# Decoder layer on one core: self attention's short products moved between long ones, the context's transpositions ahead of the output's, the queries' transpositions into the next pass

## Chip, cores and metric

The kernel runs on one core of a Trainium2 chip. The metric is the device time of one execution in microseconds. The median of three runs of the kernel before is 750.39 us (744.05 to 751.88).

## What is computed

One decoder layer on x of 8 entries x 112 tokens x 256, with a context of 8 x 375 x 256: self attention, cross attention, and a mixture of experts, each added to its input and followed by a layer norm. The change lies in the two attentions. Self attention takes its softmax over the 112 tokens of an entry, 16 heads of width 16 with rotary positions; cross attention normalises x again, has 16 heads of width 64 and 375 keys, and its output is scaled by tanh of a gate.

```python
qkv = x @ qkv_w.T + qkv_b
q, k = rotary(q), rotary(k)
attn = softmax(einsum('abhqd,abhkd->abhqk', q, k) * hd ** -0.5)
out = einsum('abhqk,bhkd->abhqd', attn, v)
out = swapaxes(out, 1, 2).reshape(B, N, D) @ proj_w.T + proj_b
x = layernorm(x + out)
xn = layernorm(x, gamma, beta)
q = xn @ w_q
k, v = split(context @ w_kv)
attn = softmax(q @ k.T * DIM_HEAD ** -0.5)
x = layernorm(x + ((attn @ v) @ w_out + b_out) * tanh(gate))
x = layernorm(x + experts(x) + shared(x))
```

The rotary factors add a leading axis a of size 1, so the swap of axes 1 and 2 ahead of self attention's projection exchanges entries and heads. The 16 x 112 x 16 numbers of two heads over all eight entries thus become the 112 x 256 input of one entry's projection. The kernel follows this: what it calls the self attention of entry b is that of heads 2b and 2b + 1 over all entries, and its result goes through DRAM once to be laid out as rows.

## The kernel before

The program has three blocks, one after the other: the preparation (weights transposed and split into a high and a low part, q, k and v of self attention with rotary), the attention block, and the experts. Every product of two fp32 operands is made of three (high x low, low x high, high x high), so that six matmuls stand for one product over a width of 256 (`product`, lines 142 to 147).

The attention block works on one entry after the other. Before its loop the first entry's self attention is made. Then `iteration(b, more)` stands once for entry 0, in a hardware loop for entries 1 to 6, and once for entry 7, which has no next entry (`more` is false). I call one iteration a pass. It has eight stages s, one for each pair of heads of cross attention. In a stage PE has the scores of pair s (`scores`, into ps_s), the key projection of a later pair (`k_project`, into ps_kt), in six of the stages a projection of values (`v_project`, into ps_vx; which one, `V_AT` says), and the product of the probabilities of pair s - 2 with the values (`pv`, into ps_o). ACT copies k's high part out of PSUM (`k_hi`), takes the exponentials with their sums (`exps`), and makes the high part of the normalised probabilities of the pair before (`p_hi`). DVE takes the negated maxima (`maxima`, c_neg) and the low parts (`k_lo`, `v_lo`, `o_lo`). POOL normalises (`normalise`: a power, a product with a scale, and a product over 112 x 750) and makes the low part of the probabilities (`p_lo`). SyncE transposes them by DMA (`transpose_p`).

Into these stages the self attention of entry b + 1, its projection, its norms and its queries are filled in pieces, the fills. Their order and the stages are written out by hand in `FILLS` and `FILL_AT`: `FILL_AT[(s, n)]` names the fills that stand at place n of stage s. On PE place 0 is behind the scores, place 1 behind the key projection, place 2 behind the value projection, place 4 behind `pv`. Every engine runs through the same table (`place(n)` in each `iteration`) for its part of a fill: PE makes it (`fill`), ACT copies or exponentiates (`fill_hi`), DVE takes maxima, low parts or moments (`fill_lo`). The fills are

- QA, QB, KA, KB: transpositions of stacked queries and keys of self attention; S0 to S3: its scores; T0 to T3: transpositions of its exponentials (128 x 112 tiles, in the profile ps_a<-ident,work);
- O0, O1: its output, 16 short matmuls each of 34 or 18 columns (ps_a<-v_self,pt_hi and pt_lo, lines 1245 and 1246), which need the low parts that DVE writes (`pt_lo`, from `self_pt`);
- OT: transposition of the output, which goes through DRAM to be laid out anew (`store_o`, `load_o` on SyncE); PJ: its projection; C0, C1: transpositions of the next context (`ctx_transpose`);
- NT: transposition of the normed x (xn); R0, R1: the query projection; Q0, Q1: transpositions of the queries (q_rows).

All fills write one of two PSUM banks (ps_a) in turn; `free(name, b)` has PE wait until the fill two places back in `FILLS` has been read. The semaphores are counted, so a fill that is moved waits for the same counts. Between PJ and NT lie two norms: DVE takes moments of x plus the output (`residual_moments`, count n1), POOL the power -0.5 (`rsqrt`), DVE norms and takes moments again (`x1_moments`, n2), POOL the second power, DVE writes xn (`xn_norm`, line 949). ACT then makes xnt_f and xnt_hi from NT (`xn_affine`, `xn_hi`), DVE the low part.

The order on every engine is that of the code. Besides the fills, the change touches the places of `store_o`, `load_o`, `load_ctx` and `load_x` on SyncE, of `residual`, `rsqrt` and `x1_out` on POOL, of `xn_hi` on ACT, and of `x1_moments`, `xn_norm` and `chunk_max` on DVE. `chunk_max` is the largest magnitude in a chunk of the experts' weights, loaded in the loop's shade.

Of the kernel before, what the change touches and what calls it, by code (L numbers as in the profile page):

```python
# [439 lines left out]
def attention_block(nc, sg, A, x2_all, ident, consts, weights, qk_rot, v_all, raw, ffn_sg, w_max, gw_raw, xs, v_cols):  # L440
# [3 lines left out]
    with ExitStack() as ctx:  # L444
# [96 lines left out]
        def _(sp):  # L541
# [62 lines left out]
            for b in range(B):  # L604
                more = b + 1 < B
                for s in range(PAIRS):
# [5 lines left out]
                    if more and s == 2:  # L612
                        store_o(b + 1)
                        load_o(b + 1)
                    if more and s == 5:
                        load_chunk(3 * b + 2)
                    if b + 2 < B and s == 5:
                        load_ctx(b + 2)
                        load_x(b + 2)
# [6 lines left out]
        def _(pool):  # L626
# [66 lines left out]
            def iteration(b, more):  # L693
                for s in range(PAIRS):
# [3 lines left out]
                    if more and s == 6:  # L698
                        rsqrt(rstd[:, 1:2], mv[:, 1, :], "n2", b + 2)
                    if s >= 1 or later(b):  # L700
                        late_p_lo(b, s)
                    normalise(b, s)
                    if more and s == 5:
                        rsqrt(rstd[:, 0:1], mv[:, 0, :], "n1", b + 2)
                    if more and s == 1:
                        residual(b + 1)
                    if more and s == 6:
# [8 lines left out]
        def _(act):  # L716
# [168 lines left out]
            def iteration(b, more):  # L885
                for s in range(PAIRS):
# [4 lines left out]

                    if more and s == 0:
# [13 lines left out]
                    place(1)  # L906
                    if s not in (1, 2, 3, 7):
# [16 lines left out]
                    if more and s == 6:  # L924
                        xn_hi(b + 1)
# [6 lines left out]
        def _(dve):  # L932
# [197 lines left out]
            def iteration(b, more):  # L1130
                for s in range(PAIRS):
                    def place(n):
                        if more:
                            for f in FILL_AT.get((s, n), ()):
                                if f != "NT":
                                    fill_lo(b + 1, f)

                    if more and s == 6:
                        x1_moments(b + 1)
                    maxima(b, s)  # L1140
                    if more and s == 6:
                        xn_norm(b + 1)
                    if more and s == 7:
                        fill_lo(b + 1, "NT")
# [19 lines left out]
                    if more and s == 7:  # L1164
                        chunk_max(3 * b + 2)
# [9 lines left out]
                    if more and s == 4:  # L1175
                        chunk_max(3 * b + 1)
                    place(4)
                    if s == 2 and later(b):
# [11 lines left out]
        def _(pe):  # L1190
            def free(name, b):

                i = FILLS.index(name)
                if name in ("PJ", "NT"):
# [61 lines left out]
            def ctx_transpose(b, k):  # L1256
                pe.wait_ge(sg["ctx_loaded"], 16 * (b + 1))
                if later(b):
# [3 lines left out]
                    else:  # L1262

                        pe.wait_ge(sg["ot_lo"], b + 1)
# [136 lines left out]
            def iteration(b, more):  # L1401
                for s in range(PAIRS):
# [6 lines left out]
                    if s == 0:  # L1409
                        k_project(b, 2)  # L1410
                    scores(b, s)
# [8 lines left out]
                    if s != 2 and s in V_AT and (s < 6 or more):  # L1420
# [728 lines left out]
```

## Time and profile before

| | |
|---|---|
| median of the runs | 750.39 us |
| profiled execution | 752.2 us |
| its span, first to last instruction | 750.4 us |
| mean granted TensorE clock | 0.876 |
| PE busy | 583.8 us (78%) |
| DVE, ACT, POOL busy | 453.9, 412.9, 379.7 us |
| scores of entry 0's first pair | from 109.5 us |
| last scores of the loop | at 545.8 us |

The attention loop takes the middle of the span; the preparation stands before it, the experts behind. A row of a timeline is: start, duration, engine, line, operation, output<-inputs, shape, count, and in brackets the idle time of the engine just before, with what ended it. PE's durations are longer than the distance between two starts, since matmuls are pipelined; the distance is what one costs.

### The profile page before, as it was taken

Reading aid. Unit: us, or ns where it says so; the run is one execution under the profiler, and the core shown is the slowest. Engines: PE = TensorE matmul, PEld = TensorE weight load, DVE = VectorE, ACT = ScalarE, POOL = GpSimd, SP = SyncE. Lnnn points to the kernel's source line nnn. Section 1 sums busy time; section 2 is a strip of 40 time slices with the busy share of each in tenths; the row PEclk is TensorE's granted clock in tenths of the full one; section 3 lists DMA queues with packets and bytes.
Section 4 is the critical chain, followed back from the end, with each engine's and each line's share of the span. In section 5 each row is a group of like instructions: output and inputs, shape, how many; then the busy total and the mean of one; then the engine's idle time right before and its main releaser. Section 6 shows DMA issues by size and latency. Waiting matters only on the chain. (4 is left out here: it accounts for less than half of the span.)

```text
span 750.4 us, 13691 instructions
## 1 busy us (share of the span) xinstructions
PE 583.8 (78%) x4362; PEld 447.3 (60%) x4362; DVE 453.9 (60%) x837; ACT 412.9 (55%) x991; POOL 379.7 (51%) x426
## 2 busy tenths in 40 slices
PE   4734677888889888988888888887436777899990
PEld 3523555767767767767767767766335454566650
DVE  3894346567667668667677567664426766833332
ACT  2434247568558568468577577564325554744431
POOL 3452026567467577477476577566541560233332
PEclk9965588989989999899999899999755899999995
DMA  8625112354353353354354344336545466533324
GB/s 220 215 89 175 27 41 66 64 97 95 67 110 83 77 110 87 73 110 110 56 104 117 62 91 111 67 74 172 128 112 202 124 214 240 127 57 58 58 35 106
DMA packets 146135, 79.37 MB, mean 106 GB/s; under 512 B 105331, under 2 KB 135283, under 8 KB 146099
## 3 DMA queue, kind: packets, MB, share of 16 engines
q1 hardware_dynamic: 141714, 72.92, 39.2%
q0 software_dynamic: 4384, 5.99, 4.8%
q8 instruction: 20, 0.33, 0.2%
q14 instruction: 17, 0.13, 0.1%
HBM read 46.74 MB, written 10.13 MB: 76 GB/s over the span
## 5 line engine op out<-in xcount | busy, mean ns | idle before, releaser
L680 POOL TENSOR_TENSOR p<-probs,p 112x750 f16<-112x750 f32 x64 | 100.5, 1571 | 64.1 <-ACT p L718 64.1
L674 POOL TENSOR_TENSOR probs<-probs,c_rcp 112x750 f32<-112x750 f32 x64 | 92.0, 1438 | 5.0
L821 ACT ACTIVATE probs<-ps_s,c_neg 112x375 f32<-112x375 f32 x128 | 72.2, 573 | 26.7 <-DVE c_neg L1043 26.5
L718 ACT ACTIVATE p<-probs 112x750 f16<-112x750 f32 x64 | 53.1, 830 | 50.1 <-POOL probs L674 50.1
L1630 POOL DMA_INDIRECT moe_sum<-gsh_hi,xs_in x21 | 33.3, 1586 | 85.6 <-ACT gsh_hi L1681 69.9
L670 POOL TENSOR_TENSOR c_rcp<-c_sum,neg_one 112x2 f32<-112x2 f32 x64 | 45.2, 706 | 59.0 <-ACT probs L821 58.7
L1043 DVE TENSOR_REDUCE c_neg<-ps_s 112x2 f32<-112x750 f32 x64 | 59.6, 932 | 12.4 <-PE ps_s L147 12.0
L1943 PE MATMUL ps_h<-w_ex,xst_hi 128*128 (+1 forms) x168 | 57.8, 386 | 2.8 <-DVE xst_lo L1720 2.7
L935 DVE TENSOR_TENSOR kt_lo<-ps_kt,kt_hi 128x376 fp32r<-128x376 f32 x64 | 34.9, 546 | 35.3 <-ACT kt_hi L718 35.3
L1038 DVE SCALAR_TENSOR_TENSOR v_lo<-ps_vx,v_scale,v_hi 128x512 f16<-128x512 f32 (+1 forms) x48 | 36.0, 750 | 33.4 <-ACT v_hi L813 33.3
L145 PE MATMUL ps_kt<-ctxt_hi,w_k_lo 128*128 128x376 f32 x128 | 53.7, 420 | 0.0
L1342 PE MATMUL ps_o<-p_t,v_lo 128*64 128x112 f16 (+1 forms) x384 | 37.0, 231 | 15.7 <-DMA p_t<-p 9.3
L147 PE MATMUL ps_kt<-ctxt_hi,w_k_hi 128*128 128x376 f32 x128 | 47.3, 369 | 0.0
L146 PE MATMUL ps_kt<-ctxt_lo,w_k_hi 128*128 128x376 f32 x128 | 47.3, 369 | 0.0
L145 PE MATMUL ps_s<-kt_hi,qt_lo 64*112 64x376 f32 x128 | 29.4, 448 | 20.5 <-ACT probs L821 17.0
L813 ACT ACTIVATE v_hi<-ps_vx,v_scale 128x512 f16<-128x512 f32 (+1 forms) x48 | 33.1, 689 | 21.2 <-PE ps_vx L147 21.1
L145 PE MATMUL ps_vx<-w_v_hi,ctxt_lo 128*128 128x512 f32 (+1 forms) x96 | 43.9, 457 | 0.6 <-DVE res L1053 0.6
L718 ACT ACTIVATE kt_hi<-ps_kt 128x376 fp32r<-128x376 f32 x64 | 30.5, 477 | 24.7 <-PE ps_kt L147 23.3
L1867 DVE TENSOR_TENSOR gsh_hi<-ps_g,gsh_hi 128x512 f16<-128x512 f32 x21 | 14.5, 690 | 47.2 <-ACT gsh_hi L1675 47.2
L1342 PEld LDWEIGHTS ps_o<-p_t,v_lo 128*64 128x64 f16 (+1 forms) x384 | 22.8, 115 | 31.4 <-DMA p_t<-p 18.6
L1083 DVE TENSOR_REDUCE w_max<-chunk 128x1024 f32 (+1 forms) x27 | 32.7, 1212 | 14.3 <-DMA chunk<-in_L_ffn_sw_dram 9.8
L146 PE MATMUL ps_vx<-w_v_lo,ctxt_hi 128*128 128x512 f32 (+1 forms) x96 | 41.2, 430 | 0.0
(307 smaller groups left out, 1805.6 us busy)
## 6 DMA issues: line engine op xcount, KB each, us to landing
chunk<-in_L_ffn_ew_dram SPq DMA_DIRECT2D x24, 512.0 KB, 3.9
spare<-in_L_ffn_ew_dram SPq DMA_DIRECT2D x18, 512.0 KB, 6.5
store<-in_L_ffn_ew_dram SPq DMA_DIRECT2D x6, 512.0 KB, 5.2
ctx_all<-in_ctx_dram SPq DMA_DIRECT2D x2, 1500.0 KB
ctx_raw<-in_ctx_dram SPq DMA_DIRECT2D x8, 375.0 KB
moe_in<-chunk SPq DMA_DIRECT2D x1, 2709.0 KB, 14.9
plain_raw<-in_L_xattn_w_kv_dram SPq DMA_DIRECT2D x2, 1024.0 KB, 15.9
xs_in<-moe_in SPq DMA_DIRECT2D x15, 129.0 KB
```

Of the source, the lines that this page charges most:

```text
L145: eng.matmul(out, ll, rh, start=start, stop=False, **kw)
L146: eng.matmul(out, lh, rl, start=False, stop=False, **kw)
L147: return eng.matmul(out, lh, rh, start=False, stop=stop, **kw)
L670: pool.tensor_tensor(c_rcp[:, s % 2, :], c_sum[:, s % 2, :], neg_one[:, :], ALU.pow).then_inc(sg["c_rcp_part"], 1)
L674: pool.tensor_tensor(probs[:, s % 2, :, :], probs[:, s % 2, :, :], c_rcp[:, s % 2, :].unsqueeze(2).to_broadcast([N, 2, SK]), ALU.mult).the ...
L680: pool.tensor_tensor(p16[:, s % 2, 1, :, 0:SK], probs[:, s % 2, :, :], p16[:, s % 2, 0, :, 0:SK], ALU.subtract)\
L718: return act.activation(dst, src, ACT.Copy)
L821: act.activation(probs[:, s % 2, h, :], ps_s[0:N, h, 0:SK], ACT.Exp, bias=c_neg[:, s % 2, h:h + 1], accum_out=c_sum[:, s % 2, h:h + 1]).th ...
L1038: dve.scalar_tensor_tensor(v[1][0:n, q, t, :], ps_v[0:n, :], v_scale[0:n, 0:1], v[0][0:n, q, t, :], op0=ALU.mult, op1=ALU.subtract).then_i ...
L1043: dve.tensor_reduce(c_neg[:, s % 2, :], ps_s[0:N, :, 0:SK], X, ALU.max, negate=True).then_inc(sg["c_neg_ready"], 1)
L1342: last = pe.matmul(ps_pv[h * CHD:(h + 1) * CHD, :], v[a][0:n_k, s // 4, t, at:at + CHD], p16_t[0:n_k, s % 2, (2 * w + h) * ST + t, :], sta ...
L1943: last = pe.matmul(out, lhs[a], rhs[b], start=start and n == 0, stop=stop and n == 2)
```

## The change

The table moves O0, T2, T3 and O1 one or more places later, puts both context transpositions at one place of stage 5, OT behind `pv` of that stage, PJ into stage 6, NT into stage 7, R0 and R1 to the end of stage 7, and takes Q0 and Q1 out of it. Those two now stand in stage 0 of the next pass, behind its key projection, and V02 follows them, ahead of the scores. The second context transposition waits for the bank's reader before it in the new order (pt_lo), and OT for the context's low parts. `store_o` and `load_o` move from stage 2 to 3 on SyncE, the loads of context and x from 5 to 6; the residual moves from stage 1 to 4 on POOL, and the norms' steps move on POOL, DVE and ACT with PJ and NT.

```diff
-           (2, 1): ["S2", "S3"], (2, 2): ["T0"], (2, 3): ["T1"], (3, 0): ["O0", "T2"],
-           (3, 1): ["T3"], (3, 2): ["O1"], (5, 1): ["OT", "C0"], (5, 4): ["C1", "PJ"],
-           (6, 4): ["NT"], (7, 2): ["R0", "R1"], (7, 4): ["Q0", "Q1"]}
+           (2, 1): ["S2", "S3"], (2, 2): ["T0"], (2, 3): ["T1"], (3, 1): ["O0", "T2"],
+           (3, 2): ["T3"], (4, 0): ["O1"], (5, 1): ["C0", "C1"], (5, 4): ["OT"], (6, 1): ["PJ"],
+           (7, 1): ["NT"], (7, 4): ["R0", "R1"]}
...
-                    if more and s == 2:
+                    if more and s == 3:
                         store_o(b + 1)
                         load_o(b + 1)
...
-                    if b + 2 < B and s == 5:
+                    if b + 2 < B and s == 6:
                         load_ctx(b + 2)
...
-                    if more and s == 6:
+                    if more and s == 7:
                         rsqrt(rstd[:, 1:2], mv[:, 1, :], "n2", b + 2)
                     if s >= 1 or later(b):
                         late_p_lo(b, s)
+                    if more and s == 6:
+                        rsqrt(rstd[:, 0:1], mv[:, 0, :], "n1", b + 2)
                     normalise(b, s)
-                    if more and s == 5:
-                        rsqrt(rstd[:, 0:1], mv[:, 0, :], "n1", b + 2)
-                    if more and s == 1:
+                    if more and s == 4:
                         residual(b + 1)
-                    if more and s == 6:
+                    if more and s == 7:
                         x1_out(b + 1)
...
+                    if s == 0 and later(b):
+                        fill_hi(b, "Q0")
+                        fill_hi(b, "Q1")
...
                     place(1)
+                    if more and s == 7:
+                        xn_hi(b + 1)
...
-                    if more and s == 6:
-                        x1_moments(b + 1)
+                    if s == 0 and later(b):
+                        fill_lo(b, "Q0")
+                        fill_lo(b, "Q1")
                     maxima(b, s)
-                    if more and s == 6:
+                    if more and s == 7:
                         xn_norm(b + 1)
...
+                    if more and s == 6:
+                        x1_moments(b + 1)
                     place(4)
+                    if more and s == 7:
+                        chunk_max(3 * b + 2)
...
+                if name == "OT" and later(b):
+                    pe.wait_ge(sg["ctxt_lo"], 2 * b + 2)
...
-                        pe.wait_ge(sg["ot_lo"], b + 1)
+                        pe.wait_ge(sg["pt_lo"], 4 * b + 4)
...
                     if s == 0:
                         k_project(b, 2)
+                        if later(b):
+                            fill(b, "Q0")
+                            fill(b, "Q1")
+                        v_project(b, V_AT[0])
                     scores(b, s)
```

Three places show what moves. The first is DVE from stage 3 to stage 4 of a pass in the loop. pt_lo are the low parts of T2 and T3, s_rcp is the first step behind O1, c_neg the maxima of the next stage's scores. Before:

```order
L966 REGISTER_ALU
L935 TENSOR_TENSOR pt_lo<-ps_a,pt_hi 112x448
L1031 REGISTER_ALU
L935 TENSOR_TENSOR kt_lo<-ps_kt,kt_hi 128x376
L935 TENSOR_TENSOR pt_lo<-ps_a,pt_hi 112x448
L1036 REGISTER_ALU
L1038 SCALAR_TENSOR_TENSOR v_lo<-ps_vx,v_scale,v_hi 128x512
L972 REGISTER_ALU
L977 RECIPROCAL s_rcp<-ps_a 112x8
```

And now:

```order
L969 REGISTER_ALU
L938 TENSOR_TENSOR pt_lo<-ps_a,pt_hi 112x448
L1039 REGISTER_ALU
L1041 SCALAR_TENSOR_TENSOR v_lo<-ps_vx,v_scale,v_hi 128x512
L938 TENSOR_TENSOR pt_lo<-ps_a,pt_hi 112x448
L938 TENSOR_TENSOR oct_lo<-ps_o,oct_hi 128x112
L1046 TENSOR_REDUCE c_neg<-ps_s 112x2
L975 REGISTER_ALU
L980 RECIPROCAL s_rcp<-ps_a 112x8
```

T3's low part, which O1 needs, now stands behind the low part of V11, and O1's reading behind the maxima of stage 4.

The second is DVE from PJ's moments on: mv is the last step of a set of moments, x the first norm, xn the second. Before, in stages 5 and 6:

```order
L1002 TENSOR_TENSOR res<-ps_a,x_res 112x256
L939 BN_STATS stats<-res 112x6
L942 BN_AGGR mv<-stats 112x2
L944 TENSOR_SCALAR mv<-mv 112x1
L949 TENSOR_SCALAR x<-res,mv,rstd 112x256
```

And now, in stages 6 and 7:

```order
L947 TENSOR_SCALAR mv<-mv 112x1
L1039 ISA
L1041 SCALAR_TENSOR_TENSOR v_lo<-ps_vx,v_scale,v_hi 128x512
L938 TENSOR_TENSOR oct_lo<-ps_o,oct_hi 128x112
L952 TENSOR_SCALAR x<-res,mv,rstd 112x256
```

The first norm stands behind the low parts of a value projection and of a pair's output.

The third is PE at the start of a pass: ps_s are the scores of stage 0, ps_vx is V02, work are QA and QB. Before:

```order
L147 MATMUL ps_s<-kt_hi,qt_hi 112x376
L1312 ISA
L145 MATMUL ps_vx<-w_v_hi,ctxt_lo 119x512
L146 MATMUL ps_vx<-w_v_lo,ctxt_hi 119x512
L147 MATMUL ps_vx<-w_v_hi,ctxt_hi 119x512
L145 MATMUL ps_vx<-w_v_hi,ctxt_lo 119x512
L146 MATMUL ps_vx<-w_v_lo,ctxt_hi 119x512
L147 MATMUL ps_vx<-w_v_hi,ctxt_hi 119x512
L1208 ISA
L1214 MATMUL ps_a<-ident,work 128x112 x4
```

And now:

```order
L1293 REGISTER_ALU
L1296 MATMUL ps_a<-ident,q_rows 128x112 x8
L1317 ISA
L145 MATMUL ps_vx<-w_v_hi,ctxt_lo 119x512
L146 MATMUL ps_vx<-w_v_lo,ctxt_hi 119x512
L147 MATMUL ps_vx<-w_v_hi,ctxt_hi 119x512
L145 MATMUL ps_vx<-w_v_hi,ctxt_lo 119x512
L146 MATMUL ps_vx<-w_v_lo,ctxt_hi 119x512
L147 MATMUL ps_vx<-w_v_hi,ctxt_hi 119x512
L1326 REGISTER_ALU
L1329 REGISTER_ALU
L145 MATMUL ps_s<-kt_hi,qt_lo 112x376
```

V02 stands ahead of the scores of stage 0 and behind the transpositions of the queries, so that nothing but QA, QB and `pv` is left between those scores and KA.

## Rows read from the trace of the kernel before

**Rows 1.** Windows of passes: length, busy per engine, PEclk, DMA share, GB/s.

```profile
280.50:335.60 55.10, 48.80 (x416) 39.71 (x416) 39.19 (x71) 37.56 (x104) 36.46 (x41) 0.94 0.43 91
335.60:390.30 54.70, 47.38 (x416) 38.06 (x417) 39.00 (x71) 37.53 (x104) 36.41 (x41) 0.97 0.43 89
...
sum 335.20, PE 294.98 PEld 238.22 DVE 234.07 ACT 226.47 POOL 219.03; mean PE 49.16 PEld 39.70 DVE 39.01 ACT 37.74 POOL 36.50
```

**Rows 2.** Waits of PE over six passes: sum in us, times, longest.

```profile
PE ps_a L1279 <- DVE xn L949: 14.0, 6, 2.4
PE ps_a L1245 <- DVE pt_lo L935: 7.2, 11, 1.0
PE ps_o L1342 <- DMA p_t<-p: 4.7, 4, 1.5
PE ps_a L1266 <- DVE ot_lo L935: 3.8, 5, 1.6
PE ps_a L1214 <- ACT q_stacked_t L739: 2.8, 6, 0.5
PE ps_s L145 <- DVE qt_lo L935: 2.8, 6, 0.6
```

**Rows 3.** Window in stages 3 and 4 of one pass, same columns.

```profile
301.00:307.80 6.80, 6.80 (x28) 6.05 (x27) 3.83 (x9) 2.57 (x7) 1.54 (x4) 0.50 0.31 68
```

**Rows 4.** Timeline of PE, stages 3 and 4: starts of O1, pv, sc, kp, V12, pv.

```profile
307.70 0.23 PE L1245 MATMUL ps_a<-v_self,pt_hi 112*112 112x34 f32 x1
...
309.34 0.24 PE L1342 MATMUL ps_o<-p_t,v_lo 128*64 128x112 f16 x2
...
309.91 0.43 PE L145 MATMUL ps_s<-kt_hi,qt_lo 64*112 64x376 f32 x2
...
310.61 0.44 PE L145 MATMUL ps_kt<-ctxt_hi,w_k_lo 128*128 128x376 f32 x1
...
311.74 0.40 PE L145 MATMUL ps_vx<-w_v_hi,ctxt_lo 128*119 128x512 f32 x1
...
313.24 0.24 PE L1342 MATMUL ps_o<-p_t,v_lo 128*64 128x112 f16 x2
```

**Rows 5.** Timeline of PE and DVE at the start of stage 3.

```profile
298.33 0.43 PE L145 MATMUL ps_s<-kt_hi,qt_lo 64*112 64x376 f32 x2
...
298.43 0.74 DVE L1038 SCALAR_TENSOR_TENSOR v_lo<-ps_vx,v_scale,v_hi 128x512 f16<-128x512 f32 x1
299.08 0.61 DVE L935 TENSOR_TENSOR pt_lo<-ps_a,pt_hi 112x448 fp32r<-112x448 f32 x1
...
301.25 0.93 DVE L1043 TENSOR_REDUCE c_neg<-ps_s 112x2 f32<-112x750 f32 x1
```

**Rows 6.** Timeline of ACT, from exps of stage 4 to exps of stage 5.

```profile
312.32 0.57 ACT L821 ACTIVATE probs<-ps_s,c_neg 112x375 f32<-112x375 f32 x1
...
313.42 0.69 ACT L813 ACTIVATE v_hi<-ps_vx,v_scale 119x512 f16<-119x512 f32 x1
...
316.21 0.83 ACT L718 ACTIVATE p<-probs 112x750 f16<-112x750 f32 x1 [1.95 <-POOL probs L674]
316.95 0.47 ACT L718 ACTIVATE kt_hi<-ps_kt 128x376 fp32r<-128x376 f32 x1
...
317.91 0.59 ACT L821 ACTIVATE probs<-ps_s,c_neg 112x375 f32<-112x375 f32 x1
```

**Rows 7.** Timeline of DVE and POOL in stage 6: the two norms.

```profile
322.33 0.41 DVE L949 TENSOR_SCALAR x<-res,mv,rstd 112x256 f32<-112x256 f32 x1 [0.80 <-POOL rstd L661]
...
323.75 0.56 POOL L661 TENSOR_TENSOR rstd<-mv,const_neg_half 112x1 f32<-112x1 f32 x1 [1.53 <-DVE mv L944]
324.28 1.56 POOL L680 TENSOR_TENSOR p<-probs,p 112x750 f16<-112x750 f32 x1
...
324.44 1.55 DVE L949 TENSOR_SCALAR xn<-x,mv,rstd 112x256 f32<-112x256 f32 x1
```

**Rows 8.** Timeline of PE in stage 0: the scores, and KA.

```profile
335.64 0.43 PE L145 MATMUL ps_s<-kt_hi,qt_lo 64*112 64x376 f32 x2 [0.46 <-DVE qt_lo L935]
...
339.81 0.41 PE L1214 MATMUL ps_a<-ident,work 112*128 112x112 f32 x2 [0.48 <-ACT q_stacked_t L739]
```

More of the change, by code:

```diff
@@ L923, in iteration @@
                     place(4)
-                    if more and s == 6:
-                        xn_hi(b + 1)
             iterations(act, iteration)
@@ L1134, in place @@
                             for f in FILL_AT.get((s, n), ()):
-                                if f != "NT":
-                                    fill_lo(b + 1, f)
-                    if more and s == 6:
-                        x1_moments(b + 1)
+                                fill_lo(b + 1, f)
+                    if s == 0 and later(b):
+                        fill_lo(b, "Q0")
+                        fill_lo(b, "Q1")
                     maxima(b, s)
-                    if more and s == 6:
+                    if more and s == 7:
                         xn_norm(b + 1)
-                    if more and s == 7:
-                        fill_lo(b + 1, "NT")
                     place(0)
@@ L1163, in iteration @@
                         v_lo_cross(b if s < 6 else b + 1, V_AT[s])
-                    if more and s == 7:
-                        chunk_max(3 * b + 2)
                     if s != 2:
@@ L1419, in iteration @@
                         cross_out(b - 1)
-                    if s != 2 and s in V_AT and (s < 6 or more):
+                    if s not in (0, 2) and s in V_AT and (s < 6 or more):
                         v_project(b if s < 6 else b + 1, V_AT[s])
```

## The prediction

> **What bounds the kernel now.** I read the windows of the attention loop's passes first, then the waits of PE inside the loop, then the timelines around the longest ones. One pass of the loop handles one batch entry and takes 335.20 / 6 = 55.87 us over six of them; PE is busy 49.16 us of it, more than any other engine, so PE sets the time and each of its waits lies on the path [rows 1]. PE loses time in two ways. It waits: the reader is to see six waits that the change touches, 14.0 + 7.2 + 4.7 + 3.8 + 2.8 + 2.8 = 35.3 us in six passes, 5.88 us a pass [rows 2]. And its clock falls: granted 0.97 in the pass that took 54.70 us, 0.94 in the mean, and 0.50 (1.2 GHz) for 6.8 us in stage 3, where PE had just waited and then run the many short products of self attention's output [rows 1, 3]. At half speed a stretch loses at most half of itself, so a pass loses at most 0.06 x 55.87 = 3.4 us to the clock.
>
> In the words below sc is a stage's scores, kp the key projection, V a value projection, pv the product with the probabilities; "stage" is one of the eight pairs of heads. At 2.4 GHz, from start to start: sc 0.70, kp 1.13, V 1.50, pv 0.57, one self output (O0 or O1) 1.64 us [rows 4].
>
> The second thing to see is a chain beside PE, the softmax of each pair. ACT runs exps, POOL normalises, ACT copies p, then k_hi, then the next exps: 312.32, 316.21, 316.95, 317.91, a step of 5.59 us in stage 5, where two small copies stand in it, and about 5.0 without them (316.95 + 0.4 - 312.32) [rows 6]. Eight steps of 5.0 are 40 us, less than a pass, so today the chain has room; but the room is in the first stages, and whatever is placed ahead of kp delays k_hi and with it the exps queued behind it on ACT.
>
> **The change part by part.** PE's instructions are the same in number and form; no engine's work is removed. So only waits and the clock can change, and I work out each wait, all in us after the start of sc in stage 3.
>
> 1. *O0 behind kp, T3 behind V11, O1 in stage 4.* O0's wait for pt_lo goes, since kp's 1.13 stands in front of it: part of the 7.2 / 6 = 1.20. O1 now needs T3's pt_lo. DVE's maximum of stage 3 ends at 302.18, 3.85 after sc [rows 5]; then ACT has exps (1.10 to the next instruction [rows 6]), T2's copy (an estimate of 0.5 from pt_lo's 0.61, the same tile on DVE) and v_hi 0.69, DVE v_lo 0.74 and pt_lo 0.61 [rows 5, 6]. The sum is 7.5. PE is ready for O1 after sc, kp, O0, T2, V11, T3, pv, sc = 0.70 + 1.13 + 1.64 + 0.45 + 1.50 + 0.45 + 0.57 + 0.70 = 7.1 (T2 and T3 estimated at 0.45 each). O1 waits 0.4 to 0.5: 1.20 becomes 0.5.
>
> 2. *O1 ahead of kp in stage 4, C0 and C1 ahead of exps in stage 5.* O1 ends at 7.5 + 1.64 = 9.2, kp at 10.3, k_hi at 10.8: only then exps of stage 4. One step later, with both context copies in it (5.7), exps of stage 5 starts at 16.5 and ends at 17.6; sc of stage 6 needs it. PE's work after O1 is kp, V, pv, sc, kp, C0 and C1 (0.75, estimated), pv, OT (0.2) = 6.55, done at 15.7. The wait, in front of OT and sc together, is 1.9. What goes: the context's wait for ot_lo, 3.8 / 6 = 0.63, and the wait for the transposed p in front of pv, 4.7 / 6 = 0.78, because SyncE now issues the transposition of p ahead of the store of the output that it had stood behind. Both are covered by the new wait. If the chain were ahead, they would be gains: bounds 0 and 1.9 for the new wait; I take 1.9, since the step of 5.59 is measured and PE has 2 us too little work to fill it.
>
> 3. *PJ in stage 6, NT in stage 7.* Both move by the same two blocks (sc and kp), so the wait of NT, 14.0 / 6 = 2.33, changes only by what its chain gains or loses. The next exps (stage 6) starts at 21.5, ends at 22.6; sc of stage 7 waits 0.25 for it. PJ's moments on DVE now stand behind k_lo, which waits for k_hi (ends 21.5) and takes 0.5: they run from 22.1 and take 1.4, as x does with its moments up to POOL's rstd (322.33 to 323.75) [rows 7]. POOL's rsqrt then stands ahead of its normalisation of stage 6, and the second rsqrt behind it: 23.5 + 0.6 + 2.7 (316.21 - 312.32 less 1.10 [rows 6]) + 0.56 [rows 7] = 27.4, then xn. For xn the rows have two prices: 1.55 where POOL's p runs beside it (324.28 to 325.84), 0.41 for the same form, x, with POOL idle [rows 7]. Behind the second rsqrt POOL's p must first get its copy from ACT (0.83 [rows 6]), so I take 0.41 and keep 1.55 for the range. NT at 27.8; PE is there at 22.6 + 0.70 + 1.13 = 24.4. The wait is 3.4, for 2.33 before. The Trainium skill, SBUF — State Buffer, section Who interferes with whom, says that GpSimd and a VectorE tensor_scalar in a two-port mode share one port pair, that the first to issue holds it for its whole instruction and that the other blocks fully. By that rule xn goes first here and 0.41 holds, as the 1.55 beside p and the 0.41 beside an idle POOL suggest; were p first, each pass would be 1.1 us longer and the total some 8 us. R0 had no wait of its own; ACT now has p, k_hi and exps of stage 7 (0.74 + 0.4 + 1.1) ahead of NT's copies and PE only V and pv (2.07) to cover it, where sc, kp and V (3.33) did. Bounds 0 and 2.2; I take 0.8.
>
> 4. *Q0 and Q1 in the next pass, V02 ahead of sc of stage 0.* The wait for qt_lo goes: 2.8 / 6 = 0.47. But KA waits for QA's copy, and on ACT that is queued behind exps of stage 0 and v_hi. From sc to KA the trace has 335.64 to 339.81, 4.17 us, with V02's 1.50 inside and a wait of 0.48 [rows 8]. ACT's part of it stays; V02 leaves. The wait becomes 0.47 + 1.50 = 2.0, bounds 1.5 (if qt's copies run earlier than the scores) and 2.5 (if ACT, which now starts the stage with them, is late by their 1 us).
>
> 5. *The rest* (residual, loads of context and x, x1_out, the moved chunk maximum) lies on POOL, SyncE and DVE with stages to spare. I cost it at nothing; its cover is that the data are read a stage or more later. If the context came late, PE would wait for it in stage 5.
>
> **The sum.** Waits touched before: 5.88 a pass. After: 0.5 + 1.9 + 0.25 + 3.4 + 0.8 + 2.0 = 8.85. That is 3.0 more a pass. The clock: two thin stretches stand apart now, which helps, but there are three waits of 1.9 to 3.4 us where there was one of that length, and the trace shows 0.50 behind such places. I leave its loss as it is, 3.4 at most, with ends of none (3.0 - 3.4 = -0.4) and half as much again (+4.7). Seven passes fill the next entry: 7 x 3.0 = 21 us. On the profiled execution's 752.2 us (span 750.4 and 1.8 around it) that gives 773; the median of the runs shown is 750.39, 1.8 lower, so I forecast 771.
>
> **The rivals.** *The clock wins* (faster). If the softmax chain keeps ahead of PE in stages 4 to 6, so that the 1.9 and the extra 1.1 at NT don't appear, the waits come out even (5.9 for 5.88) and the dense products around O0 and O1 give back most of the clock's loss, say 2.5 of 3.4: 7 x 2.5 = 17 us less, 733 on the median. The fall to 0.50 just in stage 3 speaks for it; against it speaks that from the end of kp in stage 4 the chain needs 0.5 + 5.7 + 1.1 = 7.3 us to the end of the next exps, and PE has 6.55 - 1.13 = 5.4 of work. It decides as soon as exps of stage 4 starts before about 9 us after sc of stage 3. Chance 0.19. *A wash* (no change): the waits come as worked out, the clock's loss goes: 7 x -0.4, 748, up to 757. Chance 0.16. *Worse*: xn beside p (8 us) and the clock lower behind the three waits: above 786. Chance 0.07, part of slower. *The change doesn't do what it says*: the order of PE shows O0 between kp and V and Q between kp and V02; it does.
>
> **How the numbers follow.** The forecast itself, 757 to 786, has 0.58. With the worse case slower has 0.65; about 1% (7.5 us) is what a measurement of this kernel can tell from no change; same 0.16; faster 0.19. The range goes from 737, which takes in the wash and the weaker half of the clock's case, to 786.
>
> **What would show it.** In the changed profile: PE waits of about 2 us in front of KA (on ACT's q_stacked copy), about 3 in front of NT (on xn), 1.5 to 2 in front of OT or sc of stage 6 (on ctxt_lo or exps), and none on p_t, ot_lo or qt_lo; passes of 58 to 60 us; xn at 0.4. The forecast is wrong if passes fall under 55 us with a granted clock near 1, or if the exps of stage 4 starts within 9 us of sc of stage 3.

## The result, and the profile after

The changed kernel takes 770.81 us in the median of four runs (765.25 to 775.25), beside 751.13 for the kernel before (744.05 to 753.02): a ratio of 1.0276, with a 95% interval of 1.0181 to 1.0371. It is slower, by 1.8 to 3.7%. Measured again beside the experiments it gave 1.0304 (1.0225 to 1.0382).

| | before | after | after, again |
|---|---|---|---|
| profiled execution | 752.2 us | 765.25 us | 774.06 us |
| its span | 750.4 us | 763.4 us | 772.2 us |
| mean granted clock of the span | 0.876 | 0.866 | 0.856 |
| mean of six passes of the loop | 55.87 us | 57.92 us | 59.12 us |

The windows of passes (length, busy time per engine, PEclk, DMA share, GB/s) of the changed kernel answer to [rows 1]:

```profile
167.90:225.70 57.80, 49.83 (x418) 40.07 (x418) 38.63 (x71) 37.77 (x103) 36.35 (x41) 0.91 0.40 89
341.80:399.20 57.40, 49.93 (x416) 40.29 (x416) 38.76 (x71) 37.83 (x103) 36.24 (x41) 0.91 0.40 88
...
sum 347.50, PE 299.05 PEld 240.29 DVE 232.06 ACT 226.13 POOL 217.54; mean PE 49.84 PEld 40.05 DVE 38.68 ACT 37.69 POOL 36.26
```

347.50 / 6 = 57.92 us a pass, 2.05 more than before. Seven times that is 14.4 us, and the two profiled executions are 13.0 apart: the whole difference lies in the loop. The granted clock is 0.91 in every pass; in the kernel before it is 0.91 in two of the six passes, 0.94 in three and 0.97 in one. PE stands idle for 57.92 - 49.84 = 8.08 us of a pass, 1.37 more than before (55.87 - 49.16, [rows 1]), and is busy 0.68 us longer with the same matmuls: in this profile two thirds of the loss are waits, and one third is the lower clock. PE's waits over the six passes (sum in us, times, longest), to be laid beside [rows 2]:

```profile
PE ps_a L1284 <- DVE xn L952: 14.1, 6, 2.9
PE ps_a L1219 <- ACT q_stacked_t L739: 9.7, 6, 1.7
PE ps_a L1258 <- DMA o_rows<-o_shuffle: 8.0, 4, 2.0
PE ps_a L145 <- DVE xnt_lo L938: 4.0, 6, 1.2
PE ps_a L1250 <- DVE pt_lo L938: 2.9, 6, 0.5
PE ps_a L1258 <- issue: 2.9, 2, 1.4
...
PE ps_s L145 <- DVE qt_lo L938: 1.9, 6, 0.4
PE ps_s L145 <- ACT probs L821: 1.3, 5, 0.3
```

L1284 is NT, L1219 KA, L1258 OT, L145 with xnt_lo R0, L1250 O1. The waits for p_t and ot_lo are gone, the one for pt_lo has shrunk from 7.2 to 2.9, and three have come: 10.9 us in front of OT (two rows), 9.7 in front of KA (2.8 before), 4.0 in front of R0.

The row of OT has to be read with care. It names the DMA of o_rows in four passes and nothing ("issue") in two. The timeline of one pass, from sc of stage 3: exps of stage 4 on ACT, the context's low parts on DVE, OT on PE, and further on xn and NT:

```profile
360.53 0.43 PE L145 MATMUL ps_s<-kt_hi,qt_lo 64*112 64x376 f32 x2
...
371.30 0.57 ACT L821 ACTIVATE probs<-ps_s,c_neg 112x375 f32<-112x375 f32 x1
...
376.89 0.99 DVE L938 TENSOR_TENSOR ctxt_lo<-ps_a,ctxt_hi 128x375 fp32r<-128x375 f32 x2
...
377.99 0.38 PE L1258 MATMUL ps_a<-ident,o_rows 112*128 112x112 f32 x2 [2.00 <-DMA o_rows<-o_shuffle]
...
387.94 0.42 DVE L952 TENSOR_SCALAR xn<-x,mv,rstd 112x256 f32<-112x256 f32 x1 [0.21 <-POOL rstd L661]
...
388.40 0.37 PE L1284 MATMUL ps_a<-ident,xn 112*128 112x112 f32 x1 [2.01 <-DVE xn L952]
```

ctxt_lo ends at 377.88 and OT starts 0.11 later. The load of o_rows was issued at 375.60 and the view of the DMA issues gives it 1.9 us to land, that is 377.5. The bank that OT writes, freed by ctxt_lo, came last; the DMA was only 0.4 us ahead of it. In the two passes with "issue" PE's clock fell to 0.50 behind O1's wait; there the exps of stage 4 and OT come a microsecond later. Where a wait has two causes, the row names one, and the ends of both have to be looked up.

### The profile page after: what moved, and what is told of

The parts are those of the page before. It is cut to its first block and busy times, and to the rows that moved or that the text cites. A ratio compares the mean times of both kernels' runs of the same rounds, so it can differ in the third digit from the quotient of the medians.

```text
span 763.4 us, 13709 instructions
## 1 busy us (share of the span) xinstructions
PE 586.5 (77%) x4362; PEld 448.0 (59%) x4362; DVE 451.3 (59%) x837; ACT 412.3 (54%) x991; POOL 378.4 (50%) x426
## 5 line engine op out<-in xcount | busy, mean ns | idle before, releaser
L718 ACT ACTIVATE p<-probs 112x750 f16<-112x750 f32 x64 | 53.3, 832 | 72.3 <-POOL probs L674 72.3
L670 POOL TENSOR_TENSOR c_rcp<-c_sum,neg_one 112x2 f32<-112x2 f32 x64 | 44.8, 700 | 56.8 <-ACT probs L821 56.3
L1046 DVE TENSOR_REDUCE c_neg<-ps_s 112x2 f32<-112x750 f32 x64 | 59.6, 931 | 12.1 <-PE ps_s L147 11.9
L1952 PE MATMUL ps_h<-w_ex,xst_hi 128*128 (+1 forms) x168 | 57.9, 387 | 2.8 <-DVE xst_lo L1729 2.7
L145 PE MATMUL ps_kt<-ctxt_hi,w_k_lo 128*128 128x376 f32 x128 | 53.6, 418 | 0.0
L1041 DVE SCALAR_TENSOR_TENSOR v_lo<-ps_vx,v_scale,v_hi 128x512 f16<-128x512 f32 (+1 forms) x48 | 35.9, 748 | 24.4 <-ACT v_hi L813 24.4
L145 PE MATMUL ps_vx<-w_v_hi,ctxt_lo 128*128 128x512 f32 (+1 forms) x96 | 44.9, 468 | 0.6 <-DVE res L1056 0.6
L145 PE MATMUL ps_s<-kt_hi,qt_lo 64*112 64x376 f32 x128 | 29.0, 441 | 20.9 <-ACT probs L821 18.7
L147 PE MATMUL ps_vx<-w_v_hi,ctxt_hi 128*128 128x512 f32 (+1 forms) x96 | 42.5, 442 | 0.0
L1086 DVE TENSOR_REDUCE w_max<-chunk 128x1024 f32 (+1 forms) x27 | 32.7, 1210 | 14.1 <-DMA chunk<-in_L_ffn_sw_dram 9.8
```

The costliest lines, as they stand in the source:

```text
L145: eng.matmul(out, ll, rh, start=start, stop=False, **kw)
L147: return eng.matmul(out, lh, rh, start=False, stop=stop, **kw)
L670: pool.tensor_tensor(c_rcp[:, s % 2, :], c_sum[:, s % 2, :], neg_one[:, :], ALU.pow).then_inc(sg["c_rcp_part"], 1)
L718: return act.activation(dst, src, ACT.Copy)
L1041: dve.scalar_tensor_tensor(v[1][0:n, q, t, :], ps_v[0:n, :], v_scale[0:n, 0:1], v[0][0:n, q, t, :], op0=ALU.mult, op1=ALU.subtract).then_i ...
L1046: dve.tensor_reduce(c_neg[:, s % 2, :], ps_s[0:N, :, 0:SK], X, ALU.max, negate=True).then_inc(sg["c_neg_ready"], 1)
```

## The experiments

All times of one set come with runs of the kernel before on the same chip; the ratio is the number to compare. Between versions of the changed kernel the intervals often overlap; there the rows of the profiles tell more than the times. In the diffs, `warm(out, n, width)` issues n matmuls of w_v's high part into a bank that the next real product overwrites.

**Is it the waits or the clock?** The first pair fills PE's waits with matmuls that nobody reads, in the changed kernel (e4) and in the kernel before (e5).

```diff
+            def warm(out, n, width):
+                for _ in range(n):
+                    pe.matmul(out, w_v[0][:, 0, 0:P], w_v[0][:, 0, 0:width], start=True, stop=True)
...
+                if f == "KA":
+                    pe.wait_ge(sg["kt_lo"], PAIRS * b + 3)
+                    warm(ps_k, 7, SKP)
+                elif f == "OT":
+                    pe.wait_ge(sg["v_lo"], v_no("V12", b))
+                    warm(ps_v[:, :], 6, 512)
...
```

> The changed kernel with matmuls that nobody reads put into four waits of PE: 7 of 128x376 in front of KA, 6 of 128x512 in front of OT, 8 of 128x512 in front of NT, 3 of 128x376 in front of R0 (0.2 to 0.25 us each, less than the wait each stands in). The waits end when they ended before. By the theory that a good part of the loss is the clock that falls behind the waits, the granted clock in the loop goes from 0.91 to 0.97 or more and a pass from 57.9 to 55.5 us: 754 us. By the rival (the waits themselves are the whole loss, the slow stretches lie in shade) 771 us.

> The kernel before with matmuls that nobody reads put into its waits of PE: 2 in front of KA, 2 in front of O0, 3 in front of O1, 6 ahead of pv in stage 5 (in place of the waits for p_t and ot_lo), 9 in front of NT. By the theory of the clock its loss in the loop (granted 0.943 in the mean of six passes) shrinks, but less than in the changed kernel, since the short products of O0 and O1 themselves stay where they are: 0.96 to 0.97, a pass of 55.0 instead of 55.9 us, 6 us less than the kernel before. With the changed kernel at 56.3 us a pass once its waits are filled, the changed order would still be 1.3 us a pass longer, by its waits alone. By the rival (the change is good and only the clock spoils it) the kernel before stays at 55.9 us or more, within 0.5 us of the changed one.

e4: 758.6 us, ratio 1.0225 (1.0114 to 1.0337), six passes of 56.3 us in the mean. e5: 738.7 us, ratio 0.9827 (0.9790 to 0.9864), passes of 53.7. One pass of each that ran at full clock and the one after it, first e4:

```profile
282.90:339.00 56.10, 51.23 (x440) 40.97 (x440) 38.67 (x71) 37.31 (x103) 36.25 (x41) 1.00 0.40 90
339.00:395.60 56.60, 52.47 (x440) 42.03 (x440) 38.60 (x71) 37.70 (x103) 36.26 (x41) 0.97 0.39 89
```

and e5:

```profile
272.30:325.60 53.30, 51.40 (x440) 40.69 (x440) 38.90 (x71) 37.56 (x103) 36.50 (x41) 1.00 0.45 96
325.60:379.80 54.20, 52.72 (x438) 41.89 (x438) 38.86 (x71) 37.63 (x103) 36.25 (x41) 0.97 0.44 90
```

With the clock out of the account the changed order takes 56.1 - 53.3 = 2.8 us a pass more: that is what its waits cost. The clock's share is what each kernel loses against these: 55.9 - 53.3 = 2.6 us before, 57.9 - 56.1 = 1.8 after (59.1 - 56.1 = 3.0 in the second profile, where not all of it is clock: in two passes xn stood beside POOL's p, see below). It is about the same on both sides. Both expectations were off: e4's gain was put too high, 2.4 us a pass for 1.6 (and by the ratios, 1.0225 for 1.0276, it is within the intervals), and e5's too low, 0.9 for 2.1: with the waits beside them filled, the short products of O0 and O1 no longer brought the clock down in every pass, and three of the six took 53.1 to 53.3 us.

**Which part of the change costs?** e8 has the thin products' part alone, in the kernel before and with O1 behind kp of stage 4 as in e2, not ahead of it; e10 has the late part (NT, R, Q, V02) alone. What lies between them (OT, PJ and the norms a stage later) was not run alone. The first is

```diff
-           (2, 1): ["S2", "S3"], (2, 2): ["T0"], (2, 3): ["T1"], (3, 0): ["O0", "T2"],
-           (3, 1): ["T3"], (3, 2): ["O1"], (5, 1): ["OT", "C0"], (5, 4): ["C1", "PJ"],
+           (2, 1): ["S2", "S3"], (2, 2): ["T0"], (2, 3): ["T1"], (3, 1): ["O0", "T2"],
+           (3, 2): ["T3"], (4, 1): ["O1"], (5, 1): ["C0", "OT"], (5, 4): ["C1", "PJ"],
```

and the second, with Q0 and Q1 on ACT and DVE moved accordingly,

```diff
-           (6, 4): ["NT"], (7, 2): ["R0", "R1"], (7, 4): ["Q0", "Q1"]}
+           (7, 1): ["NT"], (7, 4): ["R0", "R1"]}
...
                         k_project(b, 2)
+                        if later(b):
+                            fill(b, "Q0")
+                            fill(b, "Q1")
+                        v_project(b, V_AT[0])
```

> The kernel before with the first part of the change alone: O0 and T2 behind the key projection of stage 3, T3 behind V11, O1 in stage 4 (behind the key projection, as in e2), and C0 ahead of OT so that OT can wait for its DMA; norms, NT, R and Q stay. By the theory of the waits OT waits 1.5 to 2 us for o_rows, the waits for pt_lo (1.2 a pass) and p_t (0.8) go, and sc of stage 6 comes 17.7 us after sc of stage 3, for 19.5 without loss of clock and 21.0 in the mean of before; NT's wait stays near 2.3: a pass of 53 to 54 us, 738 us, ratio 0.98. By the rival (the norms' chain takes it back, as in e3 and e7) NT's wait grows to 4 us and a pass stays at 55.5 to 56: ratio 1.00.

> The kernel before with the last part of the change alone: NT behind the key projection of stage 7, R0 and R1 behind pv of stage 7, Q0 and Q1 in stage 0 of the next pass with V02 behind them, ahead of the scores; thin products, OT, PJ and the norms stay. By the theory of the waits NT's wait of 2.3 goes to 0.5, but KA's grows from 0.5 to 1.6 and R0 waits 0.7 to 1.2 for xnt_lo: no gain, a pass of 55.9 to 56.5 us, ratio 1.00 to 1.01. By the rival (this part costs the whole loss) a pass of 58 us, ratio 1.02.

> The changed kernel itself on the chip of e8 to e10, to compare with. Ratio to the kernel before 1.028 (1.018 to 1.037), a pass of 57.9 us, waits as in its first profile. If the ratio is under 1.015, a part of the first difference was the phase of the clock and not the order.

e8: 746.6 us, ratio 0.9894 (0.9827 to 0.9962): the thin part alone is about 1% faster, with passes of 54.7 us. e10: 790.1 us, ratio 1.0499 (1.0432 to 1.0565), passes of 60.8: the late part is worse than its rival said. The whole change measured beside them stands at 1.0304, with passes of 59.1 us where 57.9 were expected. PE's waits of e8,

```profile
PE ps_o L1342 <- DMA p_t<-p: 11.9, 6, 3.0
PE ps_a L1253 <- DMA o_rows<-o_shuffle: 10.0, 6, 1.8
PE ps_a L1279 <- DVE xn L949: 6.7, 6, 1.9
```

and of e10:

```profile
PE ps_a L145 <- DVE xnt_lo L938: 20.8, 6, 3.7
PE ps_s L145 <- ACT probs L821: 13.1, 10, 2.2
PE ps_a L1217 <- ACT q_stacked_t L739: 9.7, 6, 1.6
```

In e8 the waits change their places more than their sum: pt_lo's 7.2 and half of NT's 14.0 go, p_t grows from 4.7 to 11.9, and o_rows is new [rows 2]. In e10 NT's wait goes altogether and R0 waits 3.5 us a pass for xnt_lo instead; the scores of stage 7 now wait for the exponentials (2.2), which NT's wait had covered; KA waits 1.6. The two parts don't simply add up: e10 leaves the norms where they were, and the changed kernel, which moves them, waits 0.67 us in front of R0 and at most 0.22 in front of the scores of stage 7.

e9 is e8 with the waits filled.

> As e8, with matmuls that nobody reads in front of KA (2), OT (6) and NT (9). By the theory that the clock takes 2 us a pass behind the waits in every order, a pass is 1 to 2 us shorter than in e8: 52 us, ratio 0.96 to 0.97, better than the 0.983 of the kernel before with filled waits. By the rival (the thin products' place alone made the clock fall, and e8 has no loss left) the same as e8.

744.95 us, ratio 0.9970 (0.9925 to 1.0015), passes of 54.5 us: by the times the rival is right, filling wins next to nothing over e8. But neither runs at full clock. The granted clock is 0.94 in e8's passes, no more than in the kernel before, and 0.97 in e9's. What the thin part changes is where the clock falls: stages 3 and 4 now run at 1.00, and the stretch at 0.50 that stood in stage 3 [rows 3] stands in stage 5, behind the waits for o_rows and p_t. Two windows of one pass of e8, and one of e9:

```profile
295.50:312.10 16.60, 14.52 (x135) 12.00 (x129) 13.41 (x27) 9.58 (x24) 9.32 (x9) 1.00 0.38 80
312.20:319.00 6.80, 5.54 (x37) 4.70 (x38) 2.65 (x8) 2.75 (x8) 2.89 (x4) 0.50 0.33 63
...
310.25:313.60 3.35, 3.19 (x29) 2.79 (x29) 0.82 (x2) 1.51 (x3) 2.29 (x3) 0.50 0.40 76
```

e9 leaves the wait for p_t unfilled (1.8 us a pass), and its fillers in front of NT end up to half a microsecond after the xn that they wait beside. So its pass is 1.2 us longer than the 53.3 of e5 and 1.4 shorter than the 55.9 of the kernel before, but how the 1.2 divide between waits and clock is not shown. The thin part takes the slow stretch out of stage 3 and pays for most of that with waits for DMA and a slow stretch in stage 5; 1.2 us a pass are left (55.9 - 54.7). (These are windows of one execution each; by its ratio e9 can't be told from the kernel before, nor from e8.)

**The terms one by one.** e1 puts V02 behind the scores of stage 0 again.

```diff
                             fill(b, "Q1")
-                        v_project(b, V_AT[0])
                     scores(b, s)
...
-                    if s not in (0, 2) and s in V_AT and (s < 6 or more):
+                    if s != 2 and s in V_AT and (s < 6 or more):
```

> The changed kernel with one part undone: V02 stands behind the scores of stage 0 again, Q0 and Q1 stay in front of them. By the theory of the waits nothing is won: KA's wait on q_stacked_t falls from 1.61 to 0.5 us, but the scores of stage 0 now follow Q1 directly and wait for qt_lo, 0.3 becomes 1.7 us; a pass stays at 57.9 us, the kernel at 771 us (767 to 775). By the rival (the move of V02 alone costs KA's wait) a pass is 1.2 us shorter, 762 us.

777.1 us, ratio 1.0477 (1.0362 to 1.0591), passes of 59.3. Nothing is won, as expected:

```profile
PE ps_a L1284 <- DVE xn L952: 20.0, 6, 4.0
PE ps_s L145 <- DVE qt_lo L938: 11.6, 7, 1.7
...
PE ps_a L1219 <- ACT q_stacked_t L739: 0.9, 2, 0.5
```

KA's wait has moved to the scores, 1.7 us for 1.6. It is Q0 and Q1 directly ahead of the scores that need a cover of 1.5 us; whether V02 is it, or KA then lacks it, comes to the same. The time lies above the 767 to 775 us expected, and NT's wait is longer than in the first profile of the changed kernel: in three of the six passes xn takes 1.55 us beside POOL's p, and NT waits 3.8 to 4.0 us; in the other three it waits 2.7 to 2.8.

e2 moves O1 behind the key projection of stage 4.

```diff
-           (3, 2): ["T3"], (4, 0): ["O1"], (5, 1): ["C0", "C1"], (5, 4): ["OT"], (6, 1): ["PJ"],
+           (3, 2): ["T3"], (4, 1): ["O1"], (5, 1): ["C0", "C1"], (5, 4): ["OT"], (6, 1): ["PJ"],
```

> The changed kernel with O1 behind the key projection of stage 4 instead of ahead of it. By the prediction's step 2 (the softmax chain) exps of stage 4 starts 9.0 us after sc of stage 3 instead of 10.8, and ctxt_lo comes 1.5 us earlier; OT then waits for o_rows, whose store and load on SyncE land at 17.0 as before, so that OT starts at 17.1 instead of 17.5: 0.4 us a pass, 768 us. By the rival (only O1's place ahead of kp made the new wait) the wait of 1.8 in front of OT goes: 758 us. By a third (OT waits for the DMA alone, and O1 read later makes it later) OT's wait grows by 0.5 and the kernel takes 774 us.

757.7 us, ratio 1.0209 (1.0110 to 1.0308), passes of 57.05. In one of them:

```profile
296.97 0.43 PE L145 MATMUL ps_s<-kt_hi,qt_lo 64*112 64x376 f32 x2
...
305.78 0.57 ACT L821 ACTIVATE probs<-ps_s,c_neg 112x375 f32<-112x375 f32 x1
...
314.03 0.32 PE L1258 MATMUL ps_a<-ident,o_rows 112*128 112x112 f32 x1 [2.11 <-DMA o_rows<-o_shuffle]
```

The exps of stage 4 start 8.8 us after sc of stage 3 (9.0 expected), and OT at 17.06 (17.1): now it waits for the DMA indeed. The step of the softmax chain holds, and the first rival falls, since OT's wait does not go. The gain is 0.9 us a pass and not 0.4, because O1's own wait for pt_lo (0.48) went too, which the expectation had left out. Its passes differ much, 54.8 us at a clock of 0.97 and 59.5 at 0.89 one after the other; in the second xn stands beside POOL's p again, and NT waits 4.1 us for 2.2.

e3 lets the softmax chain ahead altogether.

```diff
-           (3, 2): ["T3"], (4, 0): ["O1"], (5, 1): ["C0", "C1"], (5, 4): ["OT"], (6, 1): ["PJ"],
+           (3, 2): ["T3"], (4, 1): ["O1"], (5, 2): ["C0", "C1"], (6, 1): ["OT"], (6, 2): ["PJ"],
```

> The changed kernel with the softmax chain let ahead: O1 behind the key projection of stage 4, C0 and C1 behind exps of stage 5 on ACT, OT behind the key projection of stage 6, PJ behind V00. By the theory of the chain sc of stage 6 starts about 15.3 us after sc of stage 3 instead of 17.8, with no wait in front of it or of OT, and NT's wait stays near 2.3, since the later exps come earlier too: 2.2 to 3 us a pass less, 750 to 756 us. By the rival (the next wait takes it over) NT's wait grows from 2.35 to about 4.5 us and the kernel stays at 767 to 771 us.

778.7 us, ratio 1.0476 (1.0361 to 1.0590). OT's wait is gone, but the next wait takes it over, as the rival said; the time lies even above its 767 to 771 us:

```profile
PE ps_a L1284 <- DVE xn L952: 22.5, 6, 3.8
PE ps_s L145 <- ACT probs L821: 9.8, 10, 1.3
PE ps_a L1219 <- ACT q_stacked_t L739: 9.7, 6, 1.6
PE ps_kt L145 <- DVE ctxt_lo L938: 4.3, 6, 0.7
```

NT waits 3.75 us a pass for 2.35: PE comes earlier, and xn, which starts from PJ, does not.

e6 and e7 shorten single waits of e2. In e6 ACT copies QA ahead of the exps of stage 0; in e7, besides, SyncE stores the output ahead of the transposition of p, DVE makes the first norm ahead of v_lo, and POOL's second rsqrt stands inside `normalise` of stage 6:

```diff
+                    if s == 0:
+                        place(2)
                     if s in (1, 3, 7):
...
+                    if more and s == 3:
+                        store_o(b + 1)
                     transpose_p(b, s)
...
+                    if more and s == 6:
+                        x1_moments(b + 1)
                     if s in V_AT and (s < 6 or more):
...
+                if more and s == 6:
+                    rsqrt(rstd[:, 1:2], mv[:, 1, :], "n2", b + 2)
                 pool.tensor_tensor(probs[:, s % 2, :, :], probs[:, s % 2, :, :],
```

> As e2 (O1 behind the key projection), and on ACT the copy of QA ahead of exps of stage 0 instead of behind exps and v_hi. By the prediction's step 4 KA waits for nothing but ACT's queue: its wait falls from 1.6 to at most 0.3 us, and with it the slow stretch that follows it in some passes: a pass 1.3 to 1.8 us shorter than the 57.0 of e2, ratio to the kernel before 1.005 (0.995 to 1.015). By the rival (exps come later by the copy's 0.55 and take it back) no change to e2: ratio 1.02.

> As e6, with OT's and NT's waits shortened where the trace of e2 shows what they wait for: store_o ahead of the transposition of p in stage 3 on SyncE, the first norm with its moments ahead of v_lo of V00 on DVE, and the second rsqrt ahead of the 1.44 us product with the scale in POOL's normalise of stage 6. By the theory of the waits OT waits 1.2 instead of 2.1 us, NT 0.7 instead of 2.2 to 2.7 us, and less clock is lost: a pass of 52 to 53 us, 20 to 25 us less than the kernel before, ratio 0.97. By the rival (what is taken off one wait comes back at the next, pv of stage 5 on p_t and R0 on xnt_lo) a pass stays at the 55.5 us of e6.

e6: 760.05 us, ratio 1.0114 (1.0072 to 1.0155), passes of 57.3, beside 57.05 in e2. By the ratio, which lies below e2's 1.0209 with overlapping intervals, a gain is possible; the passes, of the slowest of five executions, show none. KA no longer waits for ACT's queue, but for DVE:

```profile
PE ps_a L1221 <- DVE work L940: 6.1, 6, 1.0
PE ps_a L1231 <- ACT k_stacked_t L739: 6.1, 6, 1.0
```

1.6 us became 1.0 there and 1.0 in front of S0, 0.1 before: in these rows nothing is left over, as its rival said, by another link than the one it named. e7: 765.0 us, ratio 1.0193 (1.0156 to 1.0230), passes of 57.5: slower than e6. OT's wait falls to 0.6 us, and it comes back as pv on p_t and R0 on xnt_lo, with NT as long as before; the rival again:

```profile
PE ps_a L1287 <- DVE xn L955: 16.4, 6, 3.0
PE ps_a L145 <- DVE xnt_lo L941: 8.6, 6, 2.8
...
PE ps_o L1350 <- DMA p_t<-p: 4.9, 6, 0.9
```

**A version that beats both.** e11 takes from the change what paid: O0 behind the key projection, O1 behind `pv` of the same stage, so that the way through DRAM is no later than before, and the waits of KA, O1, stage 5 and NT filled.

```diff
-           (2, 1): ["S2", "S3"], (2, 2): ["T0"], (2, 3): ["T1"], (3, 0): ["O0", "T2"],
-           (3, 1): ["T3"], (3, 2): ["O1"], (5, 1): ["OT", "C0"], (5, 4): ["C1", "PJ"],
+           (2, 1): ["S2", "S3"], (2, 2): ["T0"], (2, 3): ["T1"], (3, 1): ["O0", "T2"],
+           (3, 2): ["T3"], (3, 4): ["O1"], (5, 1): ["OT", "C0"], (5, 4): ["C1", "PJ"],
```

> The kernel before with O0 and T2 behind the key projection of stage 3, T3 behind V11 and O1 behind pv of the same stage (so that the store of the output is not later than before, as it was in e8), and with unread matmuls in front of KA (2), O1 (4), behind C0 in stage 5 (6) and in front of NT (9). Norms, NT, R and Q stay. By the theory (thin products between dense ones keep the clock, as long as the output's way through DRAM isn't delayed) stage 3 shortens from the 9.7 us of e5 to 9.1, and stage 4 takes 3.9 us in every pass instead of 5.4 in half of them: a pass of 52.5 to 53 us, ratio 0.97 to 0.975. By the rival (e5 has nothing left that this moves; the softmax chain sets stage 5 anyway) the same as e5, 0.98 to 0.985.

733.96 us, ratio 0.9809 (0.9766 to 0.9853), passes of 53.0 us, at full clock through the whole loop:

```profile
272.80:325.40 52.60, 51.12 (x437) 40.53 (x437) 38.96 (x71) 37.41 (x103) 36.32 (x41) 1.00 0.46 98
325.40:378.20 52.80, 51.18 (x439) 40.59 (x439) 38.98 (x71) 37.67 (x104) 36.48 (x41) 1.00 0.46 95
```

Stage 3 takes 9.16 us and stage 4 takes 3.9 in every pass, as expected. The passes are those of the theory (52.5 to 53 us), the ratio is the one that the rival gave (0.98 to 0.985): of the 0.7 us a pass that the windows show against e5, the ratios, whose intervals overlap, can't say much. Both kernels are faster than the one before.

## Why the prediction was right, point by point

The forecast, 771 us and slower, came out at 770.8, and its mechanism is the measured one: the waits that the change makes are dearer than those it takes. That the two agree to 0.2 us is luck. The sum was 3.0 us a pass in waits with the clock's loss unchanged, 773 us for the profiled execution; that execution took 765.25, with passes 2.05 us longer, and the next profile of the same kernel has them 3.25 us longer. In the first profile the waits that the sum names come to 7.3 us a pass for the 8.85 forecast, 1.4 more than the 5.88 before and not 3.0; the rest of the 2.05 is clock. At full clock the two orders differ by 2.8 us (e4, e5), and the clock's loss is 2.6 before and 1.8 to 3.0 after.

- *Step 1, O1's wait.* 0.5 forecast, 2.9 / 6 = 0.48 measured; O0 waits for nothing. Right.
- *Step 2, OT and sc of stage 6.* exps of stage 4 start 371.30 - 360.53 = 10.77 us after sc of stage 3 (10.8), OT at 17.46 (sc of stage 6 was put at 17.6), its wait is 10.9 / 6 = 1.82 (1.9), and ctxt_lo ends it. So it is in four of the six passes; in the other two the exps start at 11.6 to 11.7 and OT at 18.4. Right, and e2 shows the cause: with O1 behind kp the chain comes 2 us earlier. The step did not say that the load of o_rows lands less than half a microsecond before, so that undoing O1's place alone wins little there.
- *Step 3, NT.* The term was mis-sized: 3.4 forecast, 14.1 / 6 = 2.35 measured. In the pass shown NT itself starts at 388.40, 27.87 after sc of stage 3 (27.8), with xn at 0.42 us. PE was late: it was put at 24.4 and was ready at 25.9, since behind OT's wait it ran at the lower of its two levels, 1.2 GHz:

```profile
378.30:381.70 3.40, 3.40 (x14) 2.93 (x14) 1.60 (x3) 1.30 (x3) 2.33 (x3) 0.50 0.53 101
```

  What the forecast booked as a wait was in part paid as clock, in four of the six passes; in the other two PE came at full clock and waited 2.9 us. xn takes 0.41 to 0.42 us in all six, with POOL idle beside it. In the second profile two of the six passes have the other price that the prediction gave; one of them:

```profile
334.36 1.56 POOL L680 TENSOR_TENSOR p<-probs,p 112x750 f16<-112x750 f32 x1
334.52 1.54 DVE L952 TENSOR_SCALAR xn<-x,mv,rstd 112x256 f32<-112x256 f32 x1
...
336.12 0.45 PE L1284 MATMUL ps_a<-ident,xn 112*128 112x112 f32 x1 [3.89 <-DVE xn L952]
```

  Here the first norm already stood beside POOL's product with the scale (x took 1.48 us), so the second rsqrt came after ACT's copy of p, and POOL started p 0.16 us ahead of xn. By the rule of the Trainium skill that the prediction cited (SBUF — State Buffer, Who interferes with whom) the first to issue holds the ports; the trace agrees, since here p was first and xn took 1.54 us. "xn goes first here" thus held in ten of the twelve passes of the two profiles.
- *Step 3, R0.* 0.8 forecast, 4.0 / 6 = 0.67 measured, in part for a reason that the step did not have: xnt_lo now runs beside POOL's product with the scale, and takes 1.47 us instead of 0.46 (below).
- *Step 4, KA.* 2.0 forecast with bounds of 1.5 and 2.5, 1.62 measured. "ACT's part of it stays" holds for the wait as it is, but ACT is not all that stands behind it: e6 finds DVE's low part 0.6 us ahead. The wait for qt_lo, said to go, stays at 0.32.
- *Step 5, the rest.* No row of the loads of context or x, or of residual, shows among PE's waits.
- *The clock.* "I leave its loss as it is" came out roughly in the sum, but hides two things that the experiments separate: the thin part takes the slow stretch out of stage 3 (e8), and the new waits bring slow stretches elsewhere (0.50 behind OT's wait, above).

*The rivals.* "The clock wins" needed exps of stage 4 within 9 us, and they came at 10.8. Its idea was sound: e8, the thin part alone, is faster by 0.4 to 1.7%. But e8 still has a granted clock of 0.94, with new waits for DMA, and e2 shows that meeting its condition (8.8 us) is not enough while the late part stays. "A wash" and "worse" did not come out as times. Half of what "worse" named did happen in part: xn met p in two passes of the second profile, while the clock did not fall by half as much again.

What the sum could not show is which part carries the loss. By its terms steps 1 and 2 saved 0.2 us a pass, and 3 and 4 cost 3.2; e8 and e10 confirm the side, with 1.2 us saved by the first part alone (with O1 behind kp) and 4.9 lost by the last alone.

## What to carry to other kernels

Ask of every product that is moved what it used to cover. Here NT, R, Q and the scores each need the one before them through copies on two other engines, and the dense blocks that stood between them (scores, two projections, pv) were their cover; a move that sets such links next to each other turns each copy into a wait, and taking one wait away then only shows the next one. Waits that can't be removed can be filled with matmuls that nobody reads: this shortens no wait, but it keeps the clock, and it made the kernel before 1.7% faster (e5). The fillers have to end before the wait does, which in e9 those in front of NT did not. And ask which engine a short step will stand beside: the same norm cost 0.41 or 1.54 us here, by whether POOL was at work.

## What the runs showed of the hardware

A subtraction of two SBUF tiles on DVE takes three times as long beside POOL. The tile xnt_lo (durations: least, median, longest in ns) in the kernel before,

```profile
L935 DVE TENSOR_TENSOR xnt_lo<-xnt_f,xnt_hi x8: 381/459/512, 101.8 to 494.6; 128x224 fp32r<-128x224 f32 x8
```

and in the changed kernel, with POOL's instruction that it runs beside:

```profile
L938 DVE TENSOR_TENSOR xnt_lo<-xnt_f,xnt_hi x8: 393/1475/1481, 100.4 to 507.6; 128x224 fp32r<-128x224 f32 x8
...
390.97 1.44 POOL L674 TENSOR_TENSOR probs<-probs,c_rcp 112x750 f32<-112x750 f32 x1
391.19 1.47 DVE L938 TENSOR_TENSOR xnt_lo<-xnt_f,xnt_hi 128x224 fp32r<-128x224 f32 x1 [1.98 <-ACT xnt_hi L783]
392.71 0.48 PE L145 MATMUL ps_a<-w_q_hi,xnt_lo 128*112 128x512 f32 x1 [0.39 <-DVE xnt_lo L938]
```

POOL's product ends at 392.41 and xnt_lo 0.25 us behind it: as if it had stood still for most of the time that POOL worked. The Trainium skill, SBUF — State Buffer, section Who interferes with whom, says that a VectorE instruction with two SBUF inputs contends with a GpSimd one that reads SBUF, and that the order of issue decides who waits; the trace agrees, with 1.47 for 0.46 us. The prediction weighed the sharing for xn alone.

Filled waits held the granted clock at 1.00 through the six passes of e11, where the kernel before has 0.91 to 0.97. And one program does not take the same time in each execution: the changed kernel's six passes took 57.9 us in the mean in one profile, at 0.91, and 59.1 in the other, at 0.89 and with xn beside POOL's p in two of them.
